# Pair matrix of a four-layer graph network read in three column parts behind counted scatters, with fp32 messages and columns stored in quads

## The chip, the cores and the metric

The kernel runs on one core of a Trainium2 chip. The metric is device time in microseconds (us). The kernel before has a median of 2275.15 us over three runs (2265.02, 2275.15 and 2275.22). One more execution was profiled; its trace is what the rows below come from.

## The reference, cut to what matters

There are 3125 nodes with 64 features and 53125 directed edges (src, dst), sorted by dst, each with a type out of 8 and a weight. Four layers follow each other, each as `x = x + layer(relu(layernorm(x)))`:

```python
# layer 0, relations
msg = einsum('nd,rdf->rnf', h, weight_r)[etype, src] / deg[dst]
M = segment_sum(msg, dst);  out = where(deg > 0, relu(0.2 * h + 0.8 * M), h)
# layer 1, attention
e = tanh(concat(h[src], h[dst]) @ W_attn.T + b_attn) @ w_out
alpha = exp(e - max per dst) / segment_sum(...);  out = segment_sum(alpha * h[src], dst)
# layer 2, Chebyshev convolution, three terms, in two gates (Z, H_tilde), started from H = 0
prop(t) = segment_sum(w * t[src], dst), w = -dis[src] * edge_weight * dis[dst]
Tx1 = prop(h);  Tx2 = 2 * prop(Tx1) - h;  out = (1 - sigmoid(Z)) * tanh(H_tilde)
# layer 3, weighted sum
support = h @ weight;  out = segment_sum(edge_weight * support[src], dst) + bias
```

## The kernel before, in words

The edges are cut into T = 416 tiles of 128 edges, one edge per partition, and the nodes into NB = 25 blocks of 128. Tiles are handled in halves of H = 8, two halves (two buffers) per iteration, IT = 26 iterations. Three stretches go over all the edges.

The **relational stretch** gathers for each tile the rows of the relation table, an indirect DMA on GpSimd (POOL, L578, one instruction per tile). The messages are split into three bf16 parts by ScalarE and VectorE (`split_messages` L627, `split_rest` L1140, `split_last` L1146), VectorE writes a bf16 one-hot of each tile's destinations over two node blocks (L1175), and TensorE (PE) adds up per tile: three parts and a column of ones against each of the two blocks (L783, L786), plus the weighted degree (L789) and the sums over duplicate (src, dst) pairs (L791). The sums stand in PSUM, one node per partition, at a block address read from a register. In the same stretch the queue of SyncE (SP) broadcasts rows of keys (L399) and writes zeros over the pair matrix (L407). At its end VectorE forms `indices` (L1211, L1215) for all 416 tiles: where in the pair matrix the weight of each pair goes.

The **pair matrix** `pairs_by_src` holds 3200 rows of EXT = 3584 fp32 cells in DRAM (28 column blocks of 128, 45.9 MB): row = source, column = destination; the last four column blocks hold the 53 last nodes and 415 extra columns for nodes whose edges begin in one tile and go on in the next ("carried" ones, folded in by 84 bf16 products). Each of 416 `scatter` instructions on POOL (L589) writes 128 cells. POOL's own order is written out by hand: gathers of relations, EARLY = 48 scatters, gathers of attention, the other 368 scatters (L593 to L605). A batch of eight scatters waits for the batch two before it to have landed.

The **attention stretch** gathers rows of the attention table (stored by SP at L519), VectorE makes transposed one-hots in two writes of 1024 bf16 columns per half (L1125), PE looks up the destination's row in three bf16 parts (L814), ScalarE makes the tanh. After a softmax whose exponents are formed for all edges at once, the **weighted stretch** multiplies the kept rows by the edges' weights, splits them again, and adds them up with the same PE code. It needs no gather, and runs beside the 368 scatters.

The **two propagations** of layer 2 are dense: `load_by_src` on SP (L418) waits for the end of the weighted stretch and for all scatters (L523 to L525), and loads the matrix by rows: five slots with the last 512 columns (1280 KB each), then 25 slots of 3072 columns (1536 KB), in a ring of four. PE multiplies (L823): scaled node rows stationary, cells moving, 512 columns per product, into seven PSUM banks, features on partitions, even and odd blocks on two halves of the array. Within the pass PE also does the extra columns and the carried part. `turn_sums` (L899) turns the sums back to nodes on partitions. Pass 1 is the same with the new rows; then come `w_last` products (L1020), gates, layernorm, and `support` (L1026 on), each over all 25 blocks before the next. SP stores the support table (L530) and only then starts `load_to_turn` (L434).

The **last product** needs the matrix with sources moving, so each 128 x 128 block of cells is transposed on PE (`turn_cells` L1050), copied out of PSUM by ScalarE and VectorE by turns (L674, L1496), and multiplied with the support rows (`use_cells` L1064). `load_to_turn` loads 4 column blocks x 4 node blocks (1024 KB) per slot in runs of 2 KB. One store of the output stands at the end (L533).

An fp32 product shows in the trace as two records, a transposition on PE as one, a bf16 product as one.

## Time and profile before

| | before |
|---|---|
| median of three runs | 2275.15 us |
| profiled execution: time / span | 2265.1 / 2263.1 us |
| TensorE matmul (PE) | 1372.3 us, 61% |
| TensorE weight load (PEld) | 985.8 us, 44% |
| VectorE (DVE) | 919.4 us, 41% |
| ScalarE (ACT) | 337.2 us, 15% |
| GpSimd (POOL) | 1269.8 us, 56% |
| DMA | 278.78 MB, mean 123 GB/s |
| mean granted TensorE clock | 0.608 of full |

Shares are of the span. POOL's busy time counts the time in which it issues an indirect DMA, about 1 us each. No engine is near full over the whole, so the stretches have to be read one by one: the page's 40 slices (56.6 us each) show which engine is dense where, the timeline names the instructions, and the chain of waits tells what the end hangs on. Marks such as L578 are lines of the kernel printed above.

### The profile page before, as it was taken

How to read it: one execution, taken by the hardware profiler on the slowest of the kernel's cores; microseconds unless marked ns; L12 is line 12 of the kernel's file. 1: busy time of each engine (PE TensorE's matmuls, PEld its weight loads, DVE VectorE, ACT ScalarE, POOL GpSimd, SP SyncE). 2: the span in 40 equal slices, each digit the busy share in tenths (PEclk: the TensorE clock that was granted, in tenths of full speed). 3: DMA queues.
4: the chain of work that ended last, by engine and by line, in shares of the span. 5: the costliest groups of instructions: out<-in, count | busy, mean ns of one | idle time of the engine just before them, and what ended most of it. 6: DMA issues, size and time to landing. Idle time of an engine off the chain costs nothing.

```text
span 2263.1 us, 41844 instructions
## 1 busy us (share of the span) xinstructions
PE 1372.3 (61%) x12594; PEld 985.8 (44%) x12595; DVE 919.4 (41%) x2741; ACT 337.2 (15%) x625; POOL 1269.8 (56%) x1278
## 2 busy tenths in 40 slices
PE   4354544545424565656564688888102878866998
PEld 2354544445423454545443466666100323434554
DVE  5566675666772322222223655555300001033333
ACT  2111111111100221112111122222000000012332
POOL 1777777777667777777777777777774000000000
PEclk8555555555555555555555555555555998987999
DMA  6555545455302323222222000000003897845775
GB/s 191 154 156 155 170 136 167 146 163 164 98 10 70 80 75 79 74 78 75 80 74 58 1 0 0 1 0 0 1 0 136 327 357 310 318 176 186 256 246 157
DMA packets 159761, 278.78 MB, mean 123 GB/s; under 512 B 44399, under 2 KB 94635, under 8 KB 153323
## 3 DMA queue, kind: packets, MB, share of 16 engines
q1 hardware_dynamic: 119658, 236.94, 30.5%
q0 software_dynamic: 40064, 41.32, 8.1%
q8 instruction: 25, 0.41, 0.1%
q14 instruction: 14, 0.11, 0.0%
HBM read 221.87 MB, written 56.29 MB: 123 GB/s over the span
## 4 chain that ended last, share of the span: by engine, by line
POOL 48%; issue 22%; PE 16%; DMA 10%; ACT 2%; DVE 1%; POOLq 0%; SPq 0%; DVEq 0%; ACTq 0%
POOL row_ring L578 29%; POOL pairs_by_src L589 19%; DMA big<-pairs_by_src 6%; PE acc L1050 4%; PE work L1064 4%; PE acc L823 4%; DMA row_ring<-attention_rows,idx_ring 3%; PE work L823 2%; ACT big L706 1%; DMA relation_rows<-big 1%; ACT big L688 1%; DMA pairs_by_src<-dup_val,idx_by_src 0%; PE work L883 0%; PE work L1081 0%; DVE stage_mem L1467 0%
## 5 line engine op out<-in xcount | busy, mean ns | idle before, releaser
L783 PE MATMUL acc<-part_ring,hot_ring 128*128 128x64 bf16 x4992 | 504.7, 238 | 350.4 <-DVE part_ring L1146 301.4
L578 POOL DMA_INDIRECT row_ring<-relation_rows,idx_ring x416 | 432.4, 1040 | 178.0 <-issue 178.0
L589 POOL DMA_INDIRECT pairs_by_src<-dup_val,idx_by_src x416 | 428.7, 1031 | 151.1 <-issue 130.4
L783 PEld LDWEIGHTS acc<-part_ring,hot_ring 128*128 128x128 bf16 x4992 | 305.9, 117 | 395.9 <-issue 361.8
L578 POOL DMA_INDIRECT row_ring<-attention_rows,idx_ring x416 | 398.2, 957 | 132.2 <-issue 119.2
L814 PE MATMUL work<-attend_mem,hot_ring 128*128 x2496 | 325.6, 232 | 216.9 <-DVE hot_ring L1125 216.0
L814 PEld LDWEIGHTS work<-attend_mem,hot_ring 128*128 128x128 bf16 x2496 | 259.7, 104 | 283.5 <-issue 224.4
L1175 DVE TENSOR_SCALAR hot_ring<-iota_bf,col_local 128x256 bf16<-128x256 bf16 x832 | 215.9, 292 | 12.8 <-DVE rest L1140 12.8
L603 POOL DMA_INDIRECT hot_ring<-support_rows,ext_node x4 | 3.8, 960 | 335.8 <-DMA support_rows<-hot_ring 334.9
L1371 DVE TENSOR_TENSOR msg<-work,row_ring 128x512 f32<-128x512 f32 x52 | 35.9, 691 | 328.6 <-DMA row_ring<-attention_rows,idx_ring 283.4
L786 PE MATMUL acc<-ones_bf,hot_ring 128*128 128x1 bf16 x832 | 159.2, 191 | 0.0
L823 PE MATMUL work<-big,attend_mem 128*64 128x512 f32 x300 | 78.9, 623 | 128.4 <-DMA big<-pairs_by_src 128.4
L786 PE MATMUL acc<-stage_mem,hot_ring 128*128 x832 | 156.7, 188 | 0.1
L823 PE MATMUL acc<-big,attend_mem 128*64 128x512 f32 x400 | 113.1, 690 | 37.7 <-DMA big<-pairs_by_src 37.6
L1496 DVE COPY big<-acc 128x512 f32<-128x512 f32 (+1 forms) x98 | 62.2, 635 | 133.6 <-PE acc L1050 133.4
L1177 DVE TENSOR_SCALAR hot_ring<-iota_bf,big 128x128 bf16<-128x128 bf16 x416 | 113.5, 275 | 0.0
L1050 PEld LDWEIGHTS acc<-ident,big 128*128 128x128 f32 x700 | 76.7, 143 | 78.2 <-issue 47.4
L1050 PE MATMUL acc<-ident,big 128*128 128x128 f32 x700 | 99.1, 283 | 11.8 <-DMA big<-pairs_by_src 11.8
L786 PEld LDWEIGHTS acc<-stage_mem,hot_ring 128*128 128x128 bf16 x832 | 89.9, 108 | 34.9 <-issue 0.4
L823 PEld LDWEIGHTS work<-big,attend_mem 128*64 128x64 f32 x300 | 26.4, 143 | 174.3 <-DMA big<-pairs_by_src 132.8
L1064 PE MATMUL work<-big,hot_ring 128*64 128x512 f32 (+1 forms) x392 | 97.2, 574 | 0.1
L789 PE MATMUL work<-hot_ring 128*128 128x75 bf16 x416 | 94.3, 227 | 0.0
(274 smaller groups left out, 1523.9 us busy)
## 6 DMA issues: line engine op xcount, KB each, us to landing
big<-pairs_by_src SPq DMA_DIRECT2D x50, 1536.0 KB, 9.7
pairs_by_src<-zeros SPq DMA_DIRECT2D x25, 1792.0 KB
big<-pairs_by_src SPq DMA_DIRECT2D x42, 1024.0 KB, 5.1
big<-key_rows SPq DMA_DIRECT2D x52, 512.0 KB
hot_ring<-local_rows SPq DMA_DIRECT2D x52, 256.0 KB, 3.4
big<-pairs_by_src SPq DMA_DIRECT2D x10, 1280.0 KB, 9.0
row_ring<-relation_rows,idx_ring POOLq DMA_INDIRECT x416
pairs_by_src<-dup_val,idx_by_src POOLq DMA_INDIRECT x416, 2.1
```

Source lines behind the costliest of these rows:

```text
L578: pool.indirect_dma_start(ring[h][:, u, 0:width], None, table, bass.IndirectOffsetOnAxis(ap=idx_ring[h][:, u:u + 1], axis=0),).then_inc(ga ...
L589: pool.indirect_dma_start(pairs_by_src, bass.IndirectOffsetOnAxis(ap=idx_by_src[:, t:t + 1], axis=0), pair_val[:, t:t + 1], None).then_inc ...
L783: m = pe.matmul(there[:, w * D:(w + 1) * D], hot, parts[h][:, u, k * D:(k + 1) * D], start=False, stop=False, skip_group_check=True)
L786: m = pe.matmul(counts_there[:, 3 * w:3 * w + n], hot, what, start=False, stop=False, skip_group_check=True)
L789: m = pe.matmul(work[0][:, 0:3 * NB], onehot_lo[h][:, u, :], hi_parts[h][:, u, :], start=False, stop=False, skip_group_check=True)
L814: m = pe.matmul(work[2 + h][:, u * D:(u + 1) * D], onehot_t[h][:, w, u * P:(u + 1) * P], there[:, (3 * w + part) * D:(3 * w + part + 1) * ...
L823: return pe.matmul(bank[half * D:(half + 1) * D, 0:w], rows_, cells, start=False, stop=False, skip_group_check=True)
L1050: t = pe.transpose(banks[n % TURNS][:, b * P:(b + 1) * P], slot_mem[:, slot % SLOTS, c:c + P], ident[:, :])
L1064: m = pe.matmul(work[g % 2][half * D:(half + 1) * D, 0:w], support[:, cb + half, :], cells_t[:, (n + half) % TURNS, 0:w], start=(cb == 0), ...
L1175: dve.tensor_scalar(onehot[h][:, u, :], iota_bf[:, :], col_local[:, col], None, ALU.is_equal)
L1177: dve.tensor_scalar(onehot_lo[h][:, u, :], iota_bf[:, 0:P], col_lo[:, col], None, ALU.is_equal)
L1496: dve.tensor_copy(cells_t[:, n % TURNS, 0:w], banks[n % TURNS][:, 0:w]).then_inc(cells_by_dve, 1)
```

## The change

It does the following; the new names are those of the diff.

- **Queue of POOL**: EARLY is 64, not 48. The indices of the first 64 tiles are formed between the last but one and the last relational iteration, those of the others behind it (`idx_ready` 1 and 2). The relation gather asks for free rows per four tiles, and PE frees them.
- **Sums**: messages stay fp32. Per tile and block of nodes one fp32 product: the 64 features and a column of ones stationary, the fp32 one-hot moving, into PSUM with features on partitions (two products per tile, in four records). The weighted stretch has the weight inside the one-hot, and ScalarE only copies rows. No splits, no products for counts. At the end the sums are copied out (four banks by ScalarE, three by VectorE) and turned by 25 products (`turn_nodes`). The attention look-up is two fp32 products per tile, with fp32 one-hots written in eight pieces of 256 columns per half. The products for degree and duplicates stay.
- **Columns of the matrix**: the first 2048 columns (16 blocks) are permuted, so that of each block the columns 0 to 31 lie in the first 512 cells of a row, 32 to 63 in the second, and so on (quads).
- **Passes**: three column parts: left (2048 columns, 13 slots of two node blocks, 2 MB), middle and right (768 columns each, 5 slots of five blocks). Pass 0 takes left, middle, right; left and middle each wait only for as many scatters as fill them (a count worked out on VectorE from the tiles' blocks, rounded up to whole pairs of batches), right waits for all. The wait for the end of the weighted stretch is gone from SP. Pass 1 takes right, left, middle. The carried part stands at the end of pass 0 and early in pass 1.
- **Between**: `w_last` products, gates, layernorm and support are done in two parts of nodes, blocks 0 to 15 and 16 to 24; part 0's products stand inside pass 1's middle part. ScalarE stores the support table, in two parts; the loads of the last product wait for free slots only.
- **Last product**: the upper 12 column blocks are transposed on PE as before (`turn_plain`), the copies all go to ScalarE. The 16 quad blocks are loaded so that each group of 32 partitions gets its quarter of the columns (4 DMAs per slot of 2 MB, 2 KB runs), transposed by VectorE in one 32 x 32 instruction per slot (13 slots, 4096 elements per partition) and used in products of 256 columns. The output is stored group by group.

```diff
-    EARLY = 48
+    SLOT = 8 * BANK
+    LEFT = TALL * P
+    SIDE = 6 * P
+    EARLY = 64
+    SPANS = {"left": (0, LEFT, LG), "middle": (LEFT, SIDE, VG), "right": (LEFT + SIDE, SIDE, VG)}
+    ORDER = (("left", "middle", "right"), ("right", "left", "middle"))
+    NODE_PARTS = (slice(0, TALL), slice(TALL, NB))
...
+            def load_pass(k, reached):
+                cells = pairs_by_src[0:CELLS, :].rearrange("(b p c) x -> p b (c x)", p=P, c=EXT)
+                n = k * PASS_SLOTS
+                for part in ORDER[k]:
+                    if reached is not None:
+                        for h in range(2):
+                            sp.wait_ge(scattered[h], reached[part])
...
+                        for q in range(QUADS):
+                            sp.dma_start(slot_mem[q * 32:(q + 1) * 32, n % SLOTS, 0:count * BANK].rearrange("p (s c) -> p s c", s=count),
+                                         quads[:, s0:s0 + count, q * BANK:(q + 1) * BANK]).then_inc(slot_here[n % SLOTS], 16)
...
-            sp.wait_ge(slot_free["agg"], FREED)
-            for h in range(2):
-                sp.wait_ge(scattered[h], 16 * T // 2)
-            n = load_by_src(0)
-            n = load_by_src(n)
-            sp.wait_ge(table_staged, 2)
-            sp.dma_start(blocks_of(support_rows), support[:, 0:NB, :]).then_inc(table_stored["gcn"], 16)
-            load_to_turn(n)
+            load_pass(0, {"left": sp.value_load(needed[0:1, 0:1], min_val=16 * H, max_val=16 * T // 2),
+                          "middle": sp.value_load(needed[0:1, 1:2], min_val=16 * H, max_val=16 * T // 2),
+                          "right": 16 * T // 2})
+            load_pass(1, None)
+            load_to_turn()
...
+            pool.wait_ge(ones_ready, 2)
             pool.wait_ge(zeroed, 16 * ZERO_STEPS)
             pool.wait_ge(idx_ready, 1)
             scatter(0, EARLY)
+            pool.wait_ge(idx_ready, 2)
             scatter(EARLY, T)
...
+            def relation_hots():
+                with dve.Fori(0, IT - 1) as it:
+                    relation_step(it)
+                dve.wait_ge(dups_read, 2 * (IT - 1))
+                indices(col_key, idx_by_src, slice(0, EARLY))
+                relation_step(IT - 1)
...
+            def turn_nodes(k):
+                pe.wait_ge(sums_by_act, (k + 1) * (MAIN // 2 + 1))
+                pe.wait_ge(sums_by_dve, (k + 1) * (MAIN // 2))
+                for b in range(NB):
+                    c = b // PER_BANK * BANK + b % PER_BANK * D1
+                    t = pe.matmul(acc[:, c:c + D1], sums_t[0:D1, b * P:(b + 1) * P], ident[0:D1, 0:D1],
+                                  start=True, stop=True, skip_group_check=True)
...
+                dve.transpose(turned_cells[:, n % TURNS, 0:rows_ * BANK].rearrange("p (b s c) -> p s b c", b=TALL, c=32),
+                              slot_mem[:, slot % SLOTS, 0:rows_ * BANK].rearrange("p (s b c) -> p s b c", b=TALL, c=32)
+                              ).then_inc(cells_turned, 1)
...
+            for g in range(NG):
+                start_rows(g)
+                for c in range(PLAIN // 4):
+                    turn_plain(g, c)
+                    if c > 0:
+                        use_plain(g, c - 1)
+                    elif g > 0:
+                        use_plain(g - 1, last)
+                    use_quads(g, c)
+                    if c == 1 and g > 0:
+                        turn_out(g - 1)
```

## Rows read from the trace of the kernel before

**Rows 1.** Page, section 2 (40 equal slices of the span): POOL's busy tenths, PE's granted clock.
```profile
POOL 1777777777667777777777777777774000000000
PEclk8555555555555555555555555555555998987999
```

**Rows 2.** Timeline of POOL: start us, busy us, engine, line, operation, count [idle before <- releaser].
```profile
50.92 1.12 POOL L578 DMA_INDIRECT row_ring<-relation_rows,idx_ring  x1 [46.33 <-issue]
...
635.77 1.00 POOL L589 DMA_INDIRECT pairs_by_src<-dup_val,idx_by_src  x1 [20.72 <-DVE idx_by_src L1215]
...
705.16 0.98 POOL L578 DMA_INDIRECT row_ring<-attention_rows,idx_ring  x1 [0.30 <-issue]
...
1235.60 1.00 POOL L589 DMA_INDIRECT pairs_by_src<-dup_val,idx_by_src  x1 [0.30 <-issue]
...
1724.33 0.96 POOL L589 DMA_INDIRECT pairs_by_src<-dup_val,idx_by_src  x1 [0.30 <-issue]
```

**Rows 3.** Chain of waits, 1724 to 1760: start us, us, what.
```profile
1724.33 7.96 DMA pairs_by_src<-dup_val,idx_by_src
```

**Rows 4.** Timeline of PE: weighted pass begins, both passes end, first turned product.
```profile
1268.60 0.34 PE L783 MATMUL acc<-part_ring,hot_ring 128*128 128x64 bf16 x3 [6.71 <-DVE part_ring L1146]
...
1875.62 5.77 PE L899 MATMUL acc<-fold_ident,big 128*128 128x64 f32 x50 [1.07 <-DVE big L1240]
...
1883.63 1.12 PE L823 MATMUL work<-big,attend_mem 128*64 128x512 f32 x2
...
2017.81 2.39 PE L1020 MATMUL acc<-w_last,big 128*128 128x128 f32 x19
...
2066.88 1.51 PE L1050 MATMUL acc<-ident,big 128*128 128x128 f32 x6 [11.77 <-DMA big<-pairs_by_src]
```

**Rows 5.** Windows: us, busy by engine (x instructions), PEclk, DMA share, GB/s.
```profile
1876.00:1881.00 5.00, 5.00 (x47) 5.00 (x46) 0.00 (x0) 0.00 (x0) 0.00 (x0) 1.00 1.05 388
1300.00:1580.00 280.00, 237.42 (x2876) 189.50 (x2876) 156.18 (x495) 56.69 (x90) 213.16 (x212) 0.50 0.02 0
2067.00:2263.00 196.00, 188.87 (x1142) 101.35 (x1142) 64.45 (x106) 57.22 (x105) 0.77 (x1) 0.98 0.72 232
```

**Rows 6.** Stores of both tables and one load: us; KB each, median us to landing.
```profile
L519 SPq DMA_DIRECT2D attention_rows<-stage_mem x1: 387/387/387, 676.2 to 676.2; - x1
...
big<-in_L_gnn_weight_r SPq DMA_DIRECT2D x2, 128.0 KB, 4.4
local_rows<-big SPq DMA_DIRECT2D x1, 128.0 KB, 2.2
```

**Rows 7.** Timeline of PE: fp32 records of 128 and 512 columns, bf16 records of 512.
```profile
662.17 3.33 PE L752 MATMUL work<-ident,Hn 128*64 128x128 f32 x16 [31.55 <-DVE Hn L1110]
...
1767.34 3.65 PE L823 MATMUL acc<-big,attend_mem 128*64 128x512 f32 x16 [0.30 <-DMA big<-pairs_by_src]
...
1790.94 5.37 PE L823 MATMUL acc<-big,row_ring 128*64 128x512 bf16 x48
```

**Rows 8.** DMA view, 1732 to 2018: GB/s in 40 slices, and the sum.
```profile
GB/s 250 392 407 428 320 365 430 239 432 299 113 389 385 356 376 232 409 375 336 282 343 7 383 425 253 380 426 248 425 286 186 378 364 386 278 370 368 394 142 0
DMA packets 13769, 91.90 MB, mean 321 GB/s; under 512 B 960, under 2 KB 960, under 8 KB 7360
```

**Rows 9.** Timeline of DVE, one instruction; page, section 5, one group of comparisons.
```profile
2032.54 1.82 DVE L1101 TENSOR_REDUCE stat<-X 128x25 f32<-128x1600 f32 x1
...
L1175 DVE TENSOR_SCALAR hot_ring<-iota_bf,col_local 128x256 bf16<-128x256 bf16 x832 | 215.9, 292 | 12.8 <-DVE rest L1140 12.8
```

**Rows 10.** Timeline of PE, 2152 to 2156; DMA view, GB/s in 40 slices, 2067 to 2263.
```profile
2152.96 1.09 PE L1050 MATMUL acc<-ident,big 128*128 128x128 f32 x8
2153.98 1.08 PE L1064 MATMUL work<-big,hot_ring 128*64 128x512 f32 x4
2154.99 1.09 PE L1050 MATMUL acc<-ident,big 128*128 128x128 f32 x8
...
GB/s 377 385 292 292 282 225 230 213 264 288 280 230 235 212 260 286 290 220 239 208 276 278 275 229 230 217 279 274 282 224 235 212 278 183 54 60 107 105 15 148
```

More of the change, by code:

```diff
@@ L726, in _ @@
[L726 to L738 removed]
+            take_extra(NG + 2, 1)
@@ new lines, in take_rows @@
+            def take_rows(g):
+                w = min(GT, NB - g * GT) * P
+                act.wait_ge(plain_used, (g + 1) * PLAIN)
+                act.wait_ge(cells_used, sum(1 for m in LAST_SLOTS if m[1] == "quad" and m[0] <= g))
+                act.activation(sums_t[:, g * BANK:g * BANK + w], work[g % 2][:, 0:w], ACT.Copy).then_inc(rows_out, 1)
+            for g in range(NG):
+                for c in range(PLAIN // 4):
+                    take_plain(g, c)
+                    if c == 0 and g > 0:
+                        take_rows(g - 1)
@@ new lines, in take_support @@
+            def take_support(part):
+                for g in groups_of(part):
+                    bs = slice(g * GT, min((g + 1) * GT, NB))
+                    n = bs.stop - bs.start
+                    dve.wait_ge(mm_done[3], g + 1)
+                    dve.tensor_copy(support[:, bs, :], banks[2 + g % 2][:, 0:n * D].rearrange("p (b c) -> p b c", b=n)
+                                    ).then_inc(mm_taken[3], 1)
+            take_banks(1, (1, 3))
+            add_last(0)
+            new_rows(0)
@@ new lines, in add_out @@
+            def add_out(g):
+                bs = slice(g * GT, min((g + 1) * GT, NB))
+                dve.wait_ge(rows_turned, g + 1)
+                dve.tensor_tensor(X[:, bs, :], X[:, bs, :], work[2 + g % 2][:, 0:(bs.stop - bs.start) * D]
+                                  .rearrange("p (b d) -> p b d", d=D), ALU.add).then_inc(sums_added, 1)
+            for n in range(len(QUAD_SLOTS)):
+                turn_quad(n)
+                if n % 2 == 1 and n >= 5:
+                    add_out(n // 2 - 2)
```

1012 lines of the change are left out of this document (562 added, 450 removed).

## The prediction, made before any run of the change

> **What bounds the kernel now.** The page's slices come first [rows 1]: until the 30th of 40 slices POOL is the one engine near full and PE is granted half its clock (1.2 GHz); behind it POOL is idle and PE's clock near full. The timeline of POOL [rows 2] says why. POOL issues 416 gathers from 50.92, 48 scatters from 635.77, 416 gathers from 705.16 and 368 scatters from 1235.60 to 1724.33, each time 0.30 us after the last instruction; its only hole is the 20.72 us ahead of 635.77. One tile costs it (635.77 − 20.72 − 50.92)/416 = 1.356 us, (705.16 − 635.77)/48 = 1.446, (1235.60 − 705.16)/416 = 1.275 and (1724.33 − 1235.60)/367 = 1.332 us in the four stretches. So up to 1725 the time is POOL's. The chain [rows 3] then waits 7.96 us for the last scatter to land, and only there do the loads of the pair matrix begin (3200 rows of 3584 fp32 cells, 45.9 MB, read three times). PE's timeline [rows 4] gives the rest: first pass up to 1883.63, second up to 2017.81, the gates, norm and support up to 2066.88, and the turned product to the end, where PE is busy 188.87 of 196 us [rows 5].
>
> **The change, part by part** (against the profiled execution: span 2263.1, time 2265.1).
>
> *1. POOL's queue.* The indices of 64 tiles are ready one relational iteration earlier, so the hole of 20.7 goes: POOL passes from its last gather to a scatter. Of the 16 scatters that move ahead of the attention gathers nothing is saved but the difference of two stretches (16 × (1.446 − 1.332) = 1.8 lost); the attention table left at 676.2 [rows 6], 30 us ahead of the first gather at 706, which covers the few us by which the new turning of the node sums (50 records, 5.8 us as in rows 4) may delay it. The one-hots become fp32. In the attention pass two writes of 1024 bf16 columns per half become eight of 256 fp32 columns. Bounds for the delay to POOL: nothing, and a tile cost of 1.446 as in the early scatters, which ran beside dense VectorE work: + 149 us over all stretches. I take + 10, since relational tiles, beside 24 such VectorE instructions per half of 8 tiles, cost only 0.08 more than attention tiles beside two. Last scatter: 1724.3 − 20.7 + 1.8 + 10 = 1715.4, landed 1723.4.
>
> *2. PE in the sums.* Ten bf16 records per tile (eight in the weighted pass) become four fp32 records and two bf16 (none). A record of 128 fp32 columns takes 3.33/16 = 0.208 us at the low clock and 2.39/19 = 0.126 at the high one [rows 1, 4, 7]; a bf16 record 280/2876 = 0.097 [rows 5]. That is 0.70 to 1.03 us per relational tile, under POOL's 1.356, and 0.50 to 0.83 in the weighted pass, which starts at 1268.6 [rows 4] and so ends between 1476 and 1613. Hidden in POOL either way. VectorE's share of a half is at most 8 × 3 comparisons at 0.292 [rows 9] and four short products, some 8 us of POOL's 10.8; the two full splits per half go there, and on ScalarE.
>
> *3. The first pass starts under the scatters.* Destinations are sorted; the inputs give 272 and 374 tiles whose first destination lies in the first 16 and 22 blocks, so the counts waited for are 272 and 384. The left part (26.2 MB) may load from 1523 (the 65th scatter starts at 1235.6 − 20.7 + 16 × 1.446 + 8 of the delay, 1246, and 208 more follow at 1.332), or at about 1620 if the weighted pass keeps the low clock; at 400 GB/s it takes 66 us, the middle part (9.8 MB) goes at 1672. Both are over by 1715. What stays behind the last scatter is the right part, 9.8 MB. The loads' rate: 321 GB/s over both passes, but 425 to 432 in slices where slots are free [rows 8]; with 2 MB slots released one by one I take 400 (320 to 430).
> After 1723.4: right part 24.6; last slot on PE (five products of 512 and five of 256 columns; 16 records of 512 take 3.65 [rows 7], so 0.45 per product of two) 3.4; the carried part, formerly beside the loads, now alone: bank copy, folds and split 5, its 84 bf16 records at 5.37/48 [rows 7] 9; last copy 0.7, turning 5.8 [rows 4], scaled rows 1.9, seams 0.6: 51 in all. Pass 2 starts at 1774.4, not 1883.6.
>
> *4. Second pass.* PE: 175 × 0.45 + 9 + 66 turnings and products of 128 columns × 0.25 + clears 2 = 106; loads: four slots are in already, 38 MB at 400 are 95. I take 107, not 134.2 (bounds 106 and 134): end 1881.
>
> *5. Between.* Before, 49.1 us, of which PE's last 11.8 wait for the first load [rows 4], now prefetched. The first 16 blocks' products, gates and norm run under the last 17 us of loads. Behind the pass remain nine of 25 blocks of the other 37.3, 13.4; VectorE's take of the first part's support stands ahead of them and waits for PE's 16 turnings and 16 products (16 × 0.13 and 16 × 0.23, 8 with seams); fixed costs of two short rounds 4: 25. PE's first plain transposition: 1906. Loads meanwhile prefetch the first group from 1875.
>
> *6. Last product.* Before, PE spends 2.03 us on 8 transpositions and 2 products [rows 10]. Now per group of four blocks: 48 transpositions and 12 products of 512 columns, six times those 2.03, 12.2; 32 products of 256 columns at half of the 0.456 of 512, with a seam 0.235, 7.5; four of 128 × 0.23, 0.9; seams 1: 21.6 us, and 135 for 25 blocks. VectorE's transposition of 4096 fp32 elements has no row. Bounds: one element per cycle as in the 1600-element pass (1.82) gives 4.4; four times that 17.5. I take 4.4, nearest to the only per-element rate shown; two per group, 9 of 21.6. The quad loads write 32 partitions at a time. Bounds: the full 400 GB/s; and 100, if a quarter of the partitions is a quarter of the way in. The nearest row, 128 KB into 64 partitions, landed in 4.4 us where 128 KB over all took 2.2 [rows 6] (runs of 256 bytes both), so I take half the best slices, 210. Then the loads bind: 26.2/0.21 + 19.7/0.4 = 174; the first 28 are prefetched, the first slot is free when VectorE has turned it (1911), so loads end at 1911 + 146 = 2057; last group 5, output 4. The span is **2066**, a gain of 197; the time 2068, and two of the three runs shown lie 10 above the profiled one: **2073**.
> The Trainium skill (SBUF — State Buffer, Door 1: The DMA port swizzle) says that 32 partitions reach 8 of 16 ports, 189 GB/s measured at 1 MiB, and that two such transfers do not add up. No row here shows a transfer into 32 partitions. By an estimate from that page's 189 the quads take 139 us, not 125, and the time would be 2087.
>
> **Rivals.**
> *A, the quad loads are not slower* (0.22). For: descriptors of 2 KB over all partitions reach 385 GB/s at the start of the last stage [rows 10]. Then PE bounds it: 1906 + 135 + 5 for the last output = 2046, up to 2051 with a first wait; time 2053 to 2058.
> *B, VectorE holds POOL up* (0.1). For: the early scatters at 1.446; against: the late ones at 1.332 beside eight comparisons per half. Attention and late tiles at 1.446: + 111 − 10; time 2170. The Trainium skill (SBUF — State Buffer, Who interferes with whom) has VectorE's two-port modes lock GpSimd out for a whole instruction, against this change's longer fp32 writes. The trace agrees only as far as the 0.11 us between 1.446 and 1.332 per scatter [rows 2].
> *C, the 32 × 32 transposition is slow or the quads load at 100 GB/s* (0.12): 13 × 17.5 = 228, or 262 + 49 less 50 of head start: time 2140 to 2170.
> *D, slower* (0.04): in the relational and weighted passes the fp32 records don't overlap with their weight loads and the clock stays low. A record then costs 0.3 (0.208 and a weight load of 101.35/1142, rows 5) to 0.42. It decides from 1.35 us per weighted tile, with which that pass ends at 1829 and the first pass, wholly behind it, eats the gain. At 0.35 a record: 1.6 per relational tile, + 101; weighted pass from 1369 to 1951, pass 2 at 1951 + 142 = 2093, time 2387. Against: rows 7 have fp32 records every 0.208 with their loads.
> *E, the counted waits bring nothing* (0.03): loads and scatters contend so that scatters of a batch of eight land more than the 10.6 us later that POOL tolerates (the last one took 7.96 [rows 3]). The first pass then costs as before, + 100: time 2168.
>
> **How the numbers follow.** Forecast 0.49, A 0.22, B 0.1, C 0.12, D 0.04, E 0.03. Range 2033 to 2155: below A's 2053 by the doubt in its PE sum, up to half of C's and short of B's; left out are D, E, most of B and some of C, and of A the least. About 0.5% (11 us) is what a measurement here can tell. Slower is D, 0.04. No change is B and E together, 2168 + 111 = 2279, 0.01 out of E's 0.03. Faster is the rest, 0.95.
>
> **What would show it.** POOL's hole ahead of the first scatter gone; first loads near 1520 (or 1620) beside scatters; pass 2 at about 1775; PE's first plain transposition near 1906; in the last stage DMA share high with GB/s well below 400 and PE waiting (forecast), or PE busy over 90% (A), or VectorE transpositions over 10 us (C). Wrong it is if POOL's last scatter lies past 1740, or the relational pass ends later than at 630.

## The result, and the profile after

The changed kernel takes 2088.01 us (median of four runs, 2085.55 to 2089.93) against 2272.83 us of the kernel before in the same comparison: a ratio of 0.9192, 95% interval 0.9166 to 0.9218. Predicted were 2073 us, faster with 0.95, and a range from 2033 to 2155. The profiled execution took 2085.55 us, its span is 2083.6.

One thing in the description ahead of the prediction is wrong, in its list and in its cut of the diff: SyncE keeps its wait for the end of the weighted pass (`slot_free["agg"]`, line 620 of the changed kernel) ahead of the first load; only the wait for all scatters went. The prediction's step 3 reckoned with a wait of that kind, and two experiments below turn on it.

The page of the kernel after, section 1 and two lines of section 2, as in [rows 1]:

```profile
PE 1301.0 (62%) x8438; PEld 1084.0 (52%) x8439; DVE 931.9 (45%) x2842; ACT 240.4 (12%) x468; POOL 1250.4 (60%) x1278
...
POOL 0777777777777777777777777777767740000000
PEclk9787778777676555555555558999596579997789
```

PE's and POOL's shares hardly moved (62% and 60%, from 61% and 56%). POOL is dense from the second slice to the 32nd. New is PE's clock: in the first ten slices it is 7 to 9 tenths and in the 25th to 28th 8 to 9, where before it was 5 from the second slice to the 30th. Three stretches in windows (columns as in [rows 5]): relational, attention, and the weighted pass:

```profile
60.00:610.00 550.00, 293.12 (x2416) 276.07 (x2417) 339.24 (x1547) 10.42 (x50) 418.03 (x406) 0.76 0.51 154
705.00:1231.00 526.00, 354.61 (x1602) 345.27 (x1601) 224.35 (x553) 98.34 (x177) 393.91 (x417) 0.50 0.29 76
1260.00:1440.00 180.00, 178.02 (x1616) 178.03 (x1617) 139.83 (x410) 32.54 (x51) 135.93 (x141) 0.99 0.02 1
```

The weighted pass runs PE 178 us of 180 at 0.99 of the full clock; before, the same pass had it busy 237 of 280 at 0.50 [rows 5]. The busy share alone doesn't give the clock: PE is busy 293 of 550 us in the relational stretch at 0.76, and 355 of 526 in the attention stretch at 0.50.

POOL's timeline, which answers to [rows 2]: first scatter, first attention gather, first late scatter, last scatter.

```profile
616.55 1.01 POOL L688 DMA_INDIRECT pairs_by_src<-dup_val,idx_by_src  x1 [0.30 <-issue]
...
705.53 0.98 POOL L677 DMA_INDIRECT rings<-attention_rows,idx_ring  x1 [0.30 <-issue]
...
1231.35 1.00 POOL L688 DMA_INDIRECT pairs_by_src<-dup_val,idx_by_src  x1 [0.30 <-issue]
...
1696.48 0.97 POOL L688 DMA_INDIRECT pairs_by_src<-dup_val,idx_by_src  x1 [0.30 <-issue]
```

The hole of 20.72 us is now the 0.30 of any other instruction. One tile costs (705.53 − 616.55)/64 = 1.390 us, (1231.35 − 705.53)/416 = 1.264 and (1696.48 − 1231.35)/351 = 1.325 in the last three stretches. The last scatter starts at 1696.5, not 1724.3, and lands 7.90 later, at 1704.4.

PE's timeline, which answers to [rows 4] (a row's count ends with the stretch that was asked for, here and below): end of the weighted pass, first left product, first middle product, end of the turned sums of pass 1, start of pass 2, first `w_last` products behind it, first plain transposition.

```profile
1439.78 5.73 PE L910 MATMUL acc<-rings 128*65 128x128 f32 x51
...
1513.88 9.19 PE L959 MATMUL acc<-big,attend_mem 128*64 128x512 f32 x32 [36.11 <-DMA big<-pairs_by_src]
...
1661.19 8.93 PE L959 MATMUL acc<-big,attend_mem 128*64 128x512 f32 x40 [85.67 <-DMA big<-pairs_by_src]
...
1750.16 5.77 PE L1047 MATMUL acc<-fold_ident,rings 128*128 128x64 f32 x50 [0.65 <-DVE rings L1451]
...
1759.23 3.68 PE L959 MATMUL acc<-big,attend_mem 128*64 128x256 f32 x13
...
1879.31 4.21 PE L1180 MATMUL acc<-w_last,rings 128*128 128x128 f32 x18 [5.01 <-DVE rings L1451]
...
1903.72 0.63 PE L1226 MATMUL acc<-ident,big 128*128 128x128 f32 x2
```

The weighted pass is over at 1445.5; the left part's loads go out at 1505.8, when 272 scatters have landed (the 272nd starts at 1503.6, and a scatter lands 2.1 us after its start in the median), and its products at 1513.9 wait for nothing but them. Middle waits 85.67 us for its count. The sums are turned by 1755.9; pass 2 starts at 1759.2 in place of 1883.6 and is over at 1874.3, before the `w_last` products of 1879.3; the last product starts at 1903.7 in place of 2066.9.

The last stage, as DMA view and as timeline of SyncE (the loads' issues) and PE:

```profile
GB/s 229 214 226 215 223 324 415 320 218 216 219 215 217 394 414 223 214 214 210 215 123 358 425 252 219 219 216 221 201 414 401 208 218 218 216 211 290 424 318 233
...
1984.54 1.27 SPq L539 DMA_DIRECT2D big<-pairs_by_src  x2
...
1985.85 0.65 SPq L534 DMA_DIRECT2D big<-pairs_by_src  x1
...
2012.29 0.39 SPq L539 DMA_DIRECT2D big<-pairs_by_src  x1
...
1962.40 0.45 PE L1226 MATMUL acc<-ident,big 128*128 128x128 f32 x1 [2.83 <-DMA big<-pairs_by_src]
...
1967.30 0.47 PE L1226 MATMUL acc<-ident,big 128*128 128x128 f32 x1 [4.24 <-DMA big<-pairs_by_src]
...
2051.23 1.12 PE L1226 MATMUL acc<-ident,big 128*128 128x128 f32 x4 [4.07 <-DMA big<-pairs_by_src]
```

The GB/s line has two levels, 215 while quads load (32 partitions each) and 415 while plain blocks do. SyncE sends the plain loads of the next group (L539) at the moment at which the last column of the group before is transposed, and PE waits for what they bring: 2.83 and 4.24 us in the third group, 4.07 in the sixth, 5.8 to 7.1 us in all in each of the groups three to six. At 2051.2 PE has the last full plain slot; the span ends 32 us later.

### The profile page after: what moved, and what is told of

Read it like the earlier page. It is cut to its first block, busy times and chain, and to the rows that moved or that the text cites. A ratio compares the mean times of both kernels' runs of the same rounds, so it can differ in the third digit from the quotient of the medians.

```text
span 2083.6 us, 29645 instructions
## 1 busy us (share of the span) xinstructions
PE 1301.0 (62%) x8438; PEld 1084.0 (52%) x8439; DVE 931.9 (45%) x2842; ACT 240.4 (12%) x468; POOL 1250.4 (60%) x1278
## 4 chain that ended last, share of the span: by engine, by line
POOL 41%; PE 20%; issue 19%; DMA 15%; ACT 2%; DVE 2%; POOLq 0%; ACTq 0%; SPq 0%; DVEq 0%
POOL rings L677 21%; POOL pairs_by_src L688 20%; PE acc L910 8%; PE acc L959 7%; DMA rings<-relation_rows,idx_ring 5%; DMA big<-pairs_by_src 5%; DMA rings<-attention_rows,idx_ring 4%; PE acc L1226 2%; ACT big L813 1%; DMA relation_rows<-big 1%; ACT big L794 1%; PE acc L916 0%; DMA pairs_by_src<-dup_val,idx_by_src 0%; PE acc L1206 0%; PE acc L1168 0%
## 5 line engine op out<-in xcount | busy, mean ns | idle before, releaser
L910 PE MATMUL acc<-rings 128*65 128x128 f32 x3328 | 475.2, 306 | 272.4 <-DMA rings<-relation_rows,idx_ring 262.8
L910 PEld LDWEIGHTS acc<-rings 128*65 128x65 f32 x3328 | 414.9, 157 | 290.9 <-issue 278.0
L677 POOL DMA_INDIRECT rings<-relation_rows,idx_ring x416 | 428.4, 1030 | 183.4 <-issue 175.5
L952 PE MATMUL acc<-attend_mem,rings 128*128 x1664 | 368.1, 423 | 179.9 <-DVE rings L1320 179.9
L677 POOL DMA_INDIRECT rings<-attention_rows,idx_ring x416 | 393.7, 946 | 132.1 <-issue 118.4
L952 PEld LDWEIGHTS acc<-attend_mem,rings 128*128 128x128 f32 x1664 | 358.8, 332 | 189.5 <-issue 189.5
L959 PE MATMUL acc<-big,attend_mem 128*64 128x512 f32 (+1 forms) x800 | 173.1, 571 | 163.0 <-DMA big<-pairs_by_src 163.0
L1377 DVE TENSOR_SCALAR rings<-iota_bf,col_local,score 128x256 f32<-128x256 bf16 x416 | 142.1, 412 | 41.6 <-PE acc L910 40.2
L1351 DVE TENSOR_SCALAR rings<-iota_bf,col_local 128x256 f32<-128x256 bf16 x416 | 151.6, 364 | 0.0
L1320 DVE TENSOR_SCALAR rings<-rings,iota_part 128x256 f32<-128x256 bf16 x416 | 128.1, 378 | 9.2 <-DMA rings<-local_rows 9.2
```

The costliest lines, as they stand in the source:

```text
L677: pool.indirect_dma_start(ring[h][:, u, 0:width], None, table, bass.IndirectOffsetOnAxis(ap=idx_ring[h][:, u:u + 1], axis=0),).then_inc(ga ...
L910: m = pe.matmul(node_sums[:, bass.ds(at[u] * P + w * P, P)], rows[h][:, u, :], onehot[h][:, u, w * P:(w + 1) * P], start=False, stop=False ...
L952: m = pe.matmul(work[2 + h][:, u * D:(u + 1) * D], onehot_t[h][:, w, u * P:(u + 1) * P], there[:, w * D:(w + 1) * D], start=(w == 0), stop ...
L959: return pe.matmul(bank[half * D:(half + 1) * D, 0:w], rows_, cells, start=False, stop=False, skip_group_check=True)
L1320: o = dve.tensor_scalar(onehot_t[h][:, w, e:e + 2 * P], local_ring[h][:, e:e + 2 * P], iota_part[:, w:w + 1], None, ALU.is_equal)
L1351: dve.tensor_scalar(onehot[h][:, u, :], iota_bf[:, :], col_local[:, col], None, ALU.is_equal)
```

## The experiments

The experiments ran on three chips, and the kernel before was measured on each: it took 2898 us on the first, 2270 on the second, much as in the comparison above, and 2893 on the third. The first and third are called slow chips here; no chip was measured twice, so that it is the chip and not the hour is likely and not shown. What differs there is told in the last section. The last stage, from the first plain transposition to the end, is nearly alike on all: where it is unedited it takes 179.9 to 182.4 us in three runs on the fast kind of chip and 182.1 to 185.2 in five on the slow ones. So it can be read everywhere, down to differences of some 5 us, while the scatters and the weighted pass can be read only on the second chip.

**The changed kernel again**, unedited, on the second chip.

> The changed kernel itself, unedited, as the measure for the others of this call, since the first experiments ran on a chip on which the kernel before took 2898 us in place of 2273 and engines other than POOL stood still for 80 us at a time in the stretch of the late scatters. Theory (that is a matter of the chip): on another chip the ratio of about 0.92 of the first measurement comes again; on the same one about 0.90, with all the other experiments beside it. Rival (it was the state of one hour): 0.92 and 2088 us everywhere.

Measured: 2089.97 us, ratio 0.9207 (0.9184 to 0.9229), within 2 us of the first comparison. The changed kernel itself did not run on the slow chips; the edit of only the waits below (2613.26 and 2601.99 us) is the nearest to it there.

**The early indices undone**, on the first chip and again on the third.

```diff
-    EARLY = 64
+    EARLY = 48
...
-                dve.wait_ge(dups_read, 2 * (IT - 1))
-                indices(col_key, idx_by_src, slice(0, EARLY))
                 relation_step(IT - 1)
...
+            indices(col_key, idx_by_src, slice(0, EARLY))
             indices(col_key, idx_by_src, slice(EARLY, T))
```

> The indices of all tiles are formed behind the last relational iteration again, and 48 scatters, not 64, stand ahead of the attention gathers. Theory (the queue of POOL ends the first half, hole and all): POOL has a hole of about 20 us ahead of its first scatter, its last scatter starts some 20 us later than 1696, and the whole is 19 to 22 us longer than with the early indices (about 2107 against 2088). Rival (the new first pass has slack that hides a part of it, since left and middle are done 17 us ahead of the last landing): the last scatter moves by 20 us, the end by under 8 us.

Measured: 2576.62 us, ratio 0.8906 (0.8875 to 0.8937). On the third chip:

> The indices formed behind the relational stretch and 48 early scatters, once more, since on the first chip the attention stretch waited 60 us longer with 64 early scatters and hid what was asked. Theory: here the hole of about 20 us ahead of the first scatter comes back and the time is 18 to 22 us above the changed kernel's, a ratio to the kernel before near 0.929. Rival (slack hides it): a ratio near 0.921.

Measured: 2577.93 us, ratio 0.8898 (0.8873 to 0.8923). This is no loss but a gain: the kernels on the same chips that keep the early indices took 2601 to 2615 us. From this run (third chip) first scatter, first attention gather and a window beside the early scatters; below them, from the run with long one-hot writes, which keeps EARLY = 64, on the same chip, the gather, a window beside the early scatters and one behind them:

```profile
694.64 1.00 POOL L688 DMA_INDIRECT pairs_by_src<-dup_val,idx_by_src  x1 [13.21 <-DVE idx_by_src L1427]
...
777.09 0.98 POOL L677 DMA_INDIRECT rings<-attention_rows,idx_ring  x1 [15.11 <-DMA attention_rows<-stage_mem]
...
710.00:730.00 20.00, 1.19 (x6) 1.01 (x7) 17.59 (x22) 0.54 (x3) 16.34 (x13) 0.50 0.02 1
```

```profile
828.61 1.14 POOL L677 DMA_INDIRECT rings<-attention_rows,idx_ring  x1 [60.48 <-DMA attention_rows<-stage_mem]
...
703.00:723.00 20.00, 0.00 (x0) 0.00 (x0) 0.00 (x0) 0.00 (x0) 15.12 (x17) 0.50 0.02 0
...
768.00:828.00 60.00, 16.58 (x90) 12.54 (x90) 32.91 (x51) 4.37 (x11) 0.13 (x1) 0.59 0.12 33
```

The hole ahead of the first scatter is there, 13.21 us. But the attention gathers start 51.5 us earlier (777.1 against 828.6). With EARLY = 64 POOL goes on to its scatters at once; the other engines do nothing at all from 703 to 743, and much of the work that the attention table needs comes behind the scatters: POOL waits 60 us for the table in place of 15. With EARLY = 48 that work does go on beside the scatters, VectorE 17.6 us of 20 in the window shown. So neither theory was met. On the fast kind of chip the effect of this part rests on the two traces (20.4 us of hole gone, nothing waited for at 705.5) and not on an experiment.

**All parts wait for all scatters**, on the first chip and again on the third.

```diff
-            load_pass(0, {"left": sp.value_load(needed[0:1, 0:1], min_val=16 * H, max_val=16 * T // 2),
-                          "middle": sp.value_load(needed[0:1, 1:2], min_val=16 * H, max_val=16 * T // 2),
+            load_pass(0, {"left": 16 * T // 2,
+                          "middle": 16 * T // 2,
```

> Left and middle wait for all the scatters, as right does; order and slots stay. Theory (counted waits hide the left and middle loads and their products under POOL): no load of the matrix before the last landing (1704), then 45.9 MB at about 400 GB/s, 115 us, and 30 us of carried part, copies and turning: pass 2 starts near 1850 in place of 1759, about 90 us longer in all (2175). Rival (the scatters beside the loads are slowed by as much as the early loads save, two batch waits of 5 us were seen): under 40 us longer.

> Left and middle wait for all the scatters, on this chip. Theory: the first load stands behind the last landing (near 1705), pass 2 starts near 1850 in place of 1759, the time is about 90 us longer (2175 to 2185). Rival (the early loads slow the scatters by much, two batch waits of 5 us were seen): under 80 us.

Measured: 2613.26 and 2601.99 us (one run each), beside 2601.30 of a run with the counts kept on the third chip. No difference, and the experiment says nothing on the counts: SyncE's first load of the matrix goes out at the same time in both, some 190 us behind the last scatter, because the weighted pass ends only there (near 2110.9 on the third chip, the last scatter starting at 1918.0). It was not run on the second chip, where the counts are at work. The tile view of the loads, first with all parts waiting, then with the counts:

```profile
L520 SPq DMA_DIRECT2D big<-pairs_by_src x46: 340/368/626, 2110.9 to 2369.2; - x46
```

```profile
L520 SPq DMA_DIRECT2D big<-pairs_by_src x46: 340/368/601, 2110.4 to 2366.2; - x46
```

The counts' worth can be read from the next run.

**The weighted products twice**, on the second chip.

```diff
+                                for _ in range(2 if key == "agg" else 1):
+                                    m = pe.matmul(node_sums[:, bass.ds(at[u] * P + w * P, P)], rows[h][:, u, :],
```

> In the weighted pass each of PE's two fp32 products per tile is done twice, so that sums and counts are both twice as large and their quotient is the same. Theory (PE's part of the weighted pass is hidden; it takes about 0.5 us per tile at full clock and ended 60 us ahead of the first load of the left part): the pass takes 200 us more, ends near 1650, the left part's loads start on their count as before, but its products (47 us) and the middle's (18) come behind and end near 1720; the right part, waited for until 1704 in any case, moves by 15 to 25 us, the whole by 15 to 25 us. Rival (the products are not hidden at all): 200 us more. Other rival (all of it is hidden): under 5 us.

Measured: 2120.64 us (one run), 31 us above the changed kernel on the same chip. Timelines of SyncE and PE, first load and start of pass 2, and the DMA view from 1630 to 1775 (slices of 3.6 us):

```profile
1632.81 0.39 SPq L520 DMA_DIRECT2D big<-pairs_by_src  x1
...
1795.01 1.55 PE L960 MATMUL acc<-big,attend_mem 128*64 128x256 f32 x6
...
GB/s 0 307 421 416 423 418 330 0 5 0 124 421 412 430 427 412 419 416 419 423 267 165 278 411 411 400 400 403 402 400 403 402 402 403 400 398 403 402 400 404
```

The pass ends near 1632, and the first load goes out there, since SyncE's wait for it was kept: 127 us later than with single products (1505.8). Pass 2 starts 36 us later. So of 127 us of delay 91 were slack. In the changed kernel the loads stand still for some 85 us ahead of the middle part and some 27 ahead of the right one, as its DMA view has it; here only for some 14, from about 1655 to 1669, since the slots are full and PE waits 18.83 us for VectorE's scaled rows behind the weighted pass, and for some 5 in three slower slices from 1702 on. From 1632.8 to the last product of the right part at 1771.4 pass 45.9 MB and 138.6 us. The same behind 1704.4, less the 14 us, since the rows would have been ready long before, would end the first pass near 1829 in place of 1735.7: the counts are worth some 93 us, an estimate from this run and not a run of their own. Of the expectation, the term of 15 to 25 was low because it forgot SyncE's wait.

**Quads over all partitions.** It leaves out the right placing of the quads' cells.

```diff
-                        for q in range(QUADS):
-                            sp.dma_start(slot_mem[q * 32:(q + 1) * 32, n % SLOTS, 0:count * BANK].rearrange("p (s c) -> p s c", s=count),
-                                         quads[:, s0:s0 + count, q * BANK:(q + 1) * BANK]).then_inc(slot_here[n % SLOTS], 16)
+                        b0 = g % 3 * 8
+                        sp.dma_start(slot_mem[:, n % SLOTS, 0:count * BANK].rearrange("p (s c) -> p s c", s=count),
+                                     wide[:, b0:b0 + count, j * BANK:(j + 1) * BANK]).then_inc(slot_here[n % SLOTS], 16)
```

> Each quad slot gets its 2 MB by one load over all 128 partitions in runs of 2 KB, in place of four loads of 32 partitions; the cells are others than the last product needs, everything else runs as before, so it leaves out the right placing of the quads. Theory (32 partitions take half the rate, 215 against 415 GB/s, and this binds the last stage): quad loads at 400 GB/s or more, a period of 23 to 25 us per group of four blocks in place of 28.9, the end 25 to 40 us earlier (about 2050 to 2063). Rival (PE's wait of some 10 us per group comes from the plain slots, which come free only with the last transposition of the group before, whatever the quads take): PE waits as long as now, under 8 us gained.

Measured on the first chip: 2601.35 us, ratio 0.8977; the last stage takes 168.9 us (2427.8 to 2596.7) where the unedited one took 182.1 and 182.9 on the same chip.

```profile
DMA  9999999900399999910099999940089999940079
GB/s 382 403 414 416 393 388 386 339 10 0 53 371 424 409 388 387 386 38 0 5 289 426 410 391 387 387 157 5 0 283 420 415 394 386 387 162 5 0 252 422
```

The loads now run at 385 to 420 GB/s, and stand still for some 9 us in each group: their rate is no bound any more, and yet only 13 us came of it. A group takes 27.1 us, where 23 to 25 were expected and the changed kernel needs 27.5 to 28.8. The rival was nearer: the plain slots come free too late, and PE still waits 5.0 us (1.7 and 3.3) for each group's plain blocks.

**Plain blocks by thirds.**

```diff
+            m = g * (PLAIN // 4) + c
+            return m, slot_mem[:, m % 4 // 2, m % 2 * (SLOT // 2):(m % 2 + 1) * (SLOT // 2)]
...
+                        for c in range(PLAIN // 4):
+                            m, place = plain_place(g, c)
...
+                                sp.wait_ge(plain_turned, (m - 3) * 4)
+                            sp.dma_start(place[:, 0:(b1 - b0) * BANK].rearrange("p (b c) -> p b c", b=b1 - b0),
+                                         plain[:, b0:b1, LEFT + c * BANK:LEFT + (c + 1) * BANK]
+                                         ).then_inc(plain_here[m % 4], 16)
```

> The 12 plain column blocks of a group are loaded as three loads of 1 MB (four column blocks of four node blocks) into a ring of four half slots, each free as soon as its third is transposed; the bytes and the quad loads stay. Theory (the loads' bytes bind the last stage: about 7.3 MB per group at a mean of 262 GB/s, 28 us): the period per group stays near 28 us, and only the tail after the last load shrinks, from 28 us to some 10: 12 to 20 us gained (2068 to 2076). Rival (the ring of plain slots binds): the period falls to 22 to 24 us and 35 us or more are gained.

Measured on the first chip: 2615.38 us, ratio 0.9039; the last stage 179.5 us, 2.6 less than the unedited one on that chip and no more than unedited stages differ among themselves.

```profile
DMA  9999999999999999999999999999999999999999
GB/s 215 221 246 389 385 300 211 222 219 214 218 221 339 386 346 211 218 216 219 220 214 206 363 386 266 214 220 221 215 223 217 230 385 375 208 218 214 223 218 220
```

The DMA engines never pause, at a mean of 256 GB/s, and the period per group stays at 28.5 to 31.4 us, from one group's first quad load to the next's: the bytes bind, as the theory had it. The tail did not shrink to some 10 us, against it: the last load lands near 2582, and the end comes 20 us behind it, where it was 26. The thirds of a group still stand behind all its quads in SyncE's queue, so that PE has nearly a whole group left to do behind them.

**Both together**, on the second chip.

> Both edits of the last stage together: plain blocks by thirds in a ring of four half slots, and each quad slot loaded over all 128 partitions (so it leaves out the right placing of the quads, as before). Alone they gave 3 and 13 us of the last stage of 182. Theory (two bounds lie at nearly the same height, the bytes of the quads at 215 GB/s and the plain slots that come free late; either alone hides what the other gives): together the loads take 17 to 19 us per group, PE is the bound, the period falls from 28 to 21.5 to 23 us and the last stage from 180 to 140 to 148 us. Rival (VectorE's transpositions and the products that wait for them bind next, at 26 us or more): the last stage stays over 160 us.

Measured: 2041.59 us, ratio 0.8981 (0.8957 to 0.9004), 48 us below the changed kernel on the same chip (again without the right placing). The last stage takes 131.8 us, where the changed kernel on this chip took 182.1: alone the edits gave 13 and 3 us (the 3 within what unedited stages differ by), together 50. PE's window over the stage, the DMA view from 1935 to 2000, and PE's timeline:

```profile
1905.00:2043.00 138.00, 131.06 (x961) 86.67 (x968) 59.50 (x24) 46.65 (x94) 3.85 (x4) 0.96 0.81 289
```

```profile
GB/s 387 389 387 387 387 387 387 386 388 387 388 382 388 387 386 384 388 387 387 387 387 389 379 387 387 388 386 387 387 387 388 386 381 389 387 387 384 388 387 389
...
1965.70 0.77 PE L1275 MATMUL acc<-fold_ident,rings 128*128 128x64 f32 x5
...
1985.38 0.88 PE L1275 MATMUL acc<-fold_ident,rings 128*128 128x64 f32 x6
```

PE is busy 131 of 138 us and a group takes 19.7 us, start of one turned output to the next. A's sum had put that price at 21.6; 21.5 to 23 were expected here.

**Two queues**, on the second chip, with the plain blocks by thirds kept.

```diff
-                        for q in range(QUADS):
+                        for q in (0, 1):
...
+                    for q in (2, 3):
+                        pool.dma_start(slot_mem[q * 32:(q + 1) * 32, n % SLOTS, 0:count * BANK].rearrange("p (s c) -> p s c", s=count),
+                                       quads[:, s0:s0 + count, q * BANK:(q + 1) * BANK]).then_inc(quad_here[n % 2], 16)
```

> Plain blocks by thirds, and of each quad slot SyncE's queue loads the partitions 0 to 63 (two loads of 32) and GpSimd's queue the partitions 64 to 127, at the same time; all is computed. Theory (the rate goes by the partitions that are open at one time, and two queues open two groups): quads at 350 to 400 GB/s, the last stage at 145 to 155 us. Rival (the loads of one queue and of the other are taken by turns by the same 16 engines, as the Trainium skill has it, SBUF — State Buffer, Can I just issue two DMAs to hit both halves?, where two gave 6% more): quads at 215 to 230 GB/s, the last stage at 172 to 182 us.

Measured: 2092.72 us, ratio 0.9210 (0.9188 to 0.9231); the last stage 178.0 us.

```profile
GB/s 254 324 353 244 248 281 250 240 212 211 201 372 391 252 254 266 254 234 209 204 214 325 390 266 254 242 252 248 217 200 220 295 388 261 257 263 261 259 223 199
```

With both queues at work the rate is 240 to 265 GB/s, then 200 to 215 when one is left. No time came of it, as the rival had it. The Trainium skill (SBUF — State Buffer, "Can I just issue two DMAs to hit both halves?") gives such a pair 6% over one load and says that they serialize; the trace shows some 17% (a mean of 255 over the slices with both queues, against 217 with one queue in the run with thirds alone), and nothing like the double.

**Dense groups**, on the third chip, the attempt at a version that beats both.

```diff
+        DENSE = (1, 3)
+        PIECES = [EB // 4 if g in DENSE else PLAIN // 4 for g in range(NG)]
...
+                    for a in range(4):
+                        for t in range(QUADS):
+                            sp.dma_start(support_q[a * 32:(a + 1) * 32, :, t, :], rows_of[a, :, t, :, :]
+                                         ).then_inc(support_q_here, 16)
```

> A version that should beat both: plain blocks by thirds, and two of the seven groups of the last product (the second and the fourth) take no quads: all their 28 column blocks come by loads over 128 partitions and are transposed on PE, the permuted ones against support rows that 16 small loads bring in the permuted order. All is computed. Theory (the bytes of the quads at 215 GB/s are the bound, and PE has 40 us to spare): a dense group costs the loads 19 us in place of 28 and PE 27 us in place of 20; the last stage falls from 180 to 155 to 165 us, the whole by 10 to 20 us (2068 to 2080). Rival (the small loads, or the wait for the support table on SyncE's queue ahead of the next loads, cost what is saved): within 5 us of 2088, or slower.

Measured: 2605.58 us, ratio 0.9004 (0.8988 to 0.9020); the last stage 180.2 us, against 182.7, 182.9 and 185.2 in the three other runs on this chip, which leave that stage alone. DMA view of the stage, and SyncE's and PE's timelines:

```profile
GB/s 216 306 389 286 64 75 108 379 299 216 229 358 271 213 216 326 336 245 124 101 289 218 252 388 275 217 304 384 215 216 283 217 250 305 203 133 115 26 0 26
...
2425.11 1.28 SPq L576 DMA_DIRECT2D attend_mem<-support_rows  x3
...
2481.88 0.45 PE L1284 MATMUL acc<-ident,big 128*128 128x128 f32 x1 [10.44 <-DMA big<-pairs_by_src]
```

The slices of 286, 64, 75 and 108 GB/s at 2415 to 2435 are the price: SyncE waits for the support table and the 16 small loads, which nothing may pass, and for some 15 us of the time when the loads are the bound they stand nearly still. Later PE waits 10.44 us for a plain piece that stands behind quads in the queue. What the dense groups save, two times 9 us by the expectation's rates, the small loads take, as far as the slices tell; no run leaves only them out. It is no better version; the changed kernel stands.

**Long one-hot writes**, on the third chip.

```diff
-                    for e in range(0, H * P, 2 * P):
-                        o = dve.tensor_scalar(onehot_t[h][:, w, e:e + 2 * P], local_ring[h][:, e:e + 2 * P],
+                    o = dve.tensor_scalar(onehot_t[h][:, w, :], local_ring[h][:, :], iota_part[:, w:w + 1], None,
```

> The fp32 one-hots of the attention stretch in two writes of 1024 columns per half in place of eight of 256. Theory (POOL's pace doesn't depend on how long one VectorE write is; a tile cost 1.264 us with eight short fp32 writes and 1.275 with two long bf16 ones): 1.26 to 1.28 us per tile. Rival (a VectorE write holds a port that POOL needs for its whole length, as the Trainium skill has it for the two-port modes, SBUF — State Buffer, Who interferes with whom): POOL waits for a part of each write of over 1 us, 1.33 us per tile or more, 30 us longer.

Measured: 2601.30 us (one run). The gathers run from 828.6 to 1448.8, 1.492 us per tile; with short writes it was 1.513 to 1.515 in the three other runs on this chip, and 1.264 to 1.267 on the fast kind of chip. So the expected numbers were missed for another reason than the one asked, and what can be compared says that long writes don't hold POOL up. They took 0.75 us each, not over 1 us as the rival had it, against 0.38 for a short one, so the test is weaker than it was meant to be. The Trainium skill (SBUF — State Buffer, Who interferes with whom) would let a long VectorE instruction in a two-port mode lock GpSimd out until it ends; no sign of it is in these numbers, taken with one run of the long form, and whether the writes ran in such a mode no row names.

## Why the prediction was right, and where it was off

Going by its own steps:

- *1, POOL's queue*: last scatter 1696.5, forecast 1715.4. The hole went as forecast, 20.4 us. The term of + 10 for VectorE's fp32 writes, with + 1.8 for the moved scatters, had the wrong sign: attention gathers (1.275 to 1.264) and late scatters (1.332 to 1.325) got cheaper by 4.6 and 2.3 us, and the 64 early scatters took 89.0 us, where 48 × 1.446 + 16 × 1.332 would be 90.7; against this the first gather started 1.9 later. Rival B is dead by that. Why they got cheaper stays open.
- *2, PE in the sums*: hidden, as forecast. The end of the weighted pass, forecast from 1476 to 1613, was 1445.5, since a tile took (1445.5 − 1262.0)/416 = 0.441 us. That is under the lower bound too: a record took 0.11 us and not 0.126. The low clock in the upper bound did not come in this pass, in which PE is busy without pauses (178 of 180 us); in the attention stretch it stayed, and what decides is not shown. D, which wanted the low clock and no overlap, is the rival that the trace contradicts most.
- *3, the first pass*: first load at 1505.8 against 1523, by POOL's earlier pace; left and middle done by 1687; behind the last landing 54.8 us, not 51. E is out: two batches of scatters waited 5.5 and 4.7 us beside the loads, no more.
- *4 and 5*: pass 2 took 115.1 us, not 107, PE busy 109.0 of them; from its end to the first plain transposition 29.4, not 25, with 7.38 us in which PE stands while VectorE forms the norm of the second part. Pass 2's term of 106 for PE was low by 3, and 6 more are PE's short waits, most of them around the turned extras.
- *6, the last product*: 179.9 us from the first plain transposition to the end, not 160, as large a miss as that of step 1. The sizes were right: 215 GB/s against 210 taken for the quads (C is out), 415 against 400, 4.45 us against 4.4 for a transposition of 4096 elements. The step that failed is "last group 5, output 4": the loads did end near 2057 (the last issued at 2049.05 took 8.4), but PE, which had the last full plain slot only at 2051.2, had a whole group and the short one to do, and the span ended 26 us behind them and not 9. A group's plain blocks are sent when the last column of the group before is transposed, and land behind its quads, so PE never gets ahead into the loads. Sending them in thirds took 6 us off this tail, no more; with fast quads as well the whole stage fell by 50.

By steps the span came out at 2066 − 19 (POOL) + 4 (first pass) + 8 (pass 2) + 4 (between) + 20 (last product) = 2083, as measured: two large errors of opposite sign, and three small ones of one sign. That the large ones cancel is luck, and by it the forecast of 2073 lies nearer to the measured 2088 than its steps do to theirs. The Trainium skill's page (SBUF — State Buffer, Door 1: The DMA port swizzle) had half the ports for 32 partitions, and the trace agrees: 215 against 415. Its 189 at 1 MiB, by which the sum came to 2087, is not the rate seen here, and that this sum fits the measured time is chance.

Rival A's condition is false (the quads are slow), and its price shows what it hid: with fast quads alone PE would not have been the bound either, since the ring of plain slots lies at nearly the same height.

## What to carry to other kernels

Two bounds of nearly the same height hide each other: take both away before either is called cheap; here 13 and 3 us became 50. For the end of a pipeline reckon what the last engine still has to do behind the last load, by the grain in which its input arrives and not by one slot. And a transfer's partitions are a size like its bytes: a layout that a faster transposition wants may cost the loads half their rate.

## What the runs showed of the hardware

The fp32 records (two per product) ran at 0.11 us each in the weighted pass with PE's clock at 0.99, where bf16 records with pauses had been granted 0.50: four longer records without gaps took 0.441 us per tile, in place of eight shorter ones and 0.78 ((1592.7 − 1268.6)/416). How much of this is the clock and how much the number of records no run separates.

The two chips on which the kernel before took 2893 and 2898 us are a second finding. There, while POOL's scatters run, the other engines hardly move in the weighted pass and for 40 us beside the early scatters. From the run with long one-hot writes, PE's timeline just behind POOL's last early scatter, whose issue ends at 768.1, and windows beside the late scatters and behind them:

```profile
769.28 0.27 PE L932 MATMUL acc<-ident,rings 65*128 65x65 f32 x1 [2.53 <-issue]
...
772.08 0.27 PE L932 MATMUL acc<-ident,rings 65*128 65x65 f32 x1 [2.53 <-issue]
...
774.89 0.47 PE L932 MATMUL acc<-ident,rings 65*128 65x65 f32 x1 [0.23 <-issue]
```

```profile
1530.00:1915.00 385.00, 51.11 (x138) 25.28 (x138) 10.87 (x32) 2.58 (x4) 290.95 (x290) 0.50 0.02 1
1970.00:2110.00 140.00, 138.89 (x1273) 138.65 (x1271) 104.68 (x313) 25.67 (x41) 0.00 (x0) 1.00 0.00 0
```

PE waits 2.53 us ahead of each of the first two records, within 4 us of the scatters, and 0.23 us ahead of one 7 us behind them; in the weighted pass it executes 138 records in 385 us beside the scatters and 1273 in 140 us when they are over. On the fast kind of chip it does the whole pass beside them. It is not so beside every scatter: with the early indices undone VectorE worked beside the early ones on the third chip, as shown above. The profile names no releaser for it ("issue"), and what differs between the chips stays open. It turns an ordering round: early indices with 16 more scatters ahead of the attention gathers go without a wait on one kind of chip and cost some 24 us on the other (2601.3 against 2577.9).
